# Local attention: the order of a head group's score matmuls on TensorE, and the place of its products with V

## The reference

```python
def local_attention(q, k, v):
    # 16 heads of 64; windows of 32 queries see the window before and their own
    bk2, bv2 = (look(bk), look(bv))
    mask = (it < jb) | (it > jb + w) | (jb == -1)
    sim = jnp.einsum('bhwie,bhwje->bhwij', bq, bk2) * QK_SCALE
    sim = jnp.where(mask, -jnp.finfo(sim.dtype).max, sim)
    attn = jax.nn.softmax(sim, -1)
    return jnp.einsum('bhwij,bhwje->bhwie', attn, bv2)

def attn_layer(x, Wqkv, qs, ksc, Wo):
    q, k, v = jnp.split(x @ Wqkv, 3, -1)
    # l2norm of q and k, scales, rotary tables, local_attention
    return out @ Wo

for i in range(DEPTH):
    x = attn_layer(shift_tokens(x), ...) + x
    x = ffn_layer(shift_tokens(x), ...) + x
```

## Time and profile before

| | us |
|---|---|
| median of 3 runs | 2675.11 (2673.16 to 2679.03) |
| the profiled execution | 2671.8 |
| its span | 2669.9 |
| TensorE busy | 2478.0 (93%) |
| VectorE busy | 1932.8 (72%) |
| ScalarE busy | 1742.4 (65%) |
| GpSimd busy | 1552.0 (58%) |
| granted clock of TensorE | 0.983 of full |

### The profile page before, as it was taken

How to read it: one execution, slowest core, us unless ns; L and a number is a source line. 1 busy time by engine, 2 the same in 40 slices (tenths; PEclk the granted TensorE clock), 3 DMA queues, 4 the chain that set the end, 5 groups by cost and what they waited for, 6 DMA issues and landing times.

```text
span 2669.9 us, 62150 instructions
## 1 busy us (share of the span) xinstructions
PE 2478.0 (93%) x22737; PEld 1645.5 (62%) x22737; DVE 1932.8 (72%) x2966; ACT 1742.4 (65%) x3296; POOL 1552.0 (58%) x1359
## 2 busy tenths in 40 slices
PE   6898699996999999999999999999999999999995
PEld 3555366663666666666666666666666666666664
DVE  4899777775777777777777777777777777777773
ACT  5888454443666766667667676676666766667663
POOL 4787523333666666566656666666656666666661
PEclk8999899998999999999999999999999999999997
DMA  2312200000221221222212212122122221222211
GB/s 73 107 63 65 73 6 1 1 1 22 53 60 48 64 65 47 60 56 61 59 48 59 66 51 59 48 61 68 47 59 53 64 59 47 60 63 54 59 48 45
DMA packets 102906, 140.33 MB, mean 53 GB/s; under 512 B 63040, under 2 KB 63936, under 8 KB 102336
## 3 DMA queue, kind: packets, MB, share of 16 engines
q1 hardware_dynamic: 102848, 139.57, 19.5%
HBM read 56.39 MB, written 1.31 MB: 22 GB/s over the span
## 4 chain that ended last, share of the span: by engine, by line
issue 31%; POOL 26%; PE 11%; DVE 5%; ACT 1%; POOLq 1%; DMA 0%; DVEq 0%; SPq 0%; ACTq 0%
POOL f_qkr L1358 8%; POOL f_qkr L1365 5%; POOL f_Pr L1340 5%; POOL f_qkr L1357 5%; DVE f_m L1554 4%; PE f_psA L1723 4%; PE f_psD L1817 3%; POOL f_tab L1348 2%; PE f_psO L1707 2%; PE f_psP L1686 2%; ACT f_sq L1432 1%; POOL xall L1379 1%; POOLq L1348 0%; POOLq L1379 0%; PE f_psD L1727 0%
## 5 line engine op out<-in xcount | busy, mean ns | idle before, releaser
L1340 POOL TENSOR_TENSOR f_Pr<-f_Pr,f_rden 128x384 f32<-128x384 f32 x384 | 310.6, 829 | 696.4 <-DVE f_rden L1533 696.4
L1554 DVE TENSOR_TENSOR f_m<-f_psA,f_tab 128x1024 f32<-128x1024 f32 x384 | 452.5, 1220 | 245.7 <-ACT f_sq L1432 245.7
L1723 PE MATMUL f_psA<-f_W,f_xT 128*128 (+1 forms) x1152 | 605.2, 618 | 17.2 <-issue 10.5
L1365 POOL TENSOR_TENSOR f_qkr<-f_qkr,f_rn 128x1024 f32<-128x1024 f32 x192 | 360.9, 1900 | 0.3 <-DVE f_rn L1583 0.3
L1432 ACT ACTIVATE f_sq<-f_psA 128x512 f32<-128x512 f32 x384 | 228.8, 596 | 145.5 <-PE f_psA L1723 139.7
L1686 PEld LDWEIGHTS f_psP<-ident,f_Pr 128*96 128x96 f32 x1536 | 165.3, 126 | 218.9 <-POOL f_Pr L1340 152.3
L1407 ACT ACTIVATE f_PT<-f_psP 96x512 f32<-96x512 f32 x384 | 226.7, 590 | 86.3 <-PE f_psP L1686 74.9
L1357 POOL TENSOR_TENSOR f_qkr<-f_m 128x512 f32<-128x512 f32 x192 | 244.3, 1272 | 57.2 <-DVE f_m L1554 57.1
L1723 PEld LDWEIGHTS f_psA<-f_W,f_xT 128*128 128x128 f32 x1152 | 183.5, 196 | 141.5 <-issue 64.0
L1707 PE MATMUL f_psO<-f_PT,f_V 96*64 96x64 f32 x6144 | 263.8, 228 | 3.3
L1522 DVE TENSOR_REDUCE f_mx<-f_psS 128x8 f32<-128x768 f32 x192 | 179.7, 936 | 118.1 <-PE f_psS L1670 118.1
(11 more groups left out here) (160 smaller groups left out, 4440.2 us busy)
## 6 DMA issues: line engine op xcount, KB each, us to landing
f_V<-f_Vt SPq DMA_DIRECT2D x96, 384.0 KB, 4.2
f_V<-f_Vt SPq DMA_DIRECT2D x96, 256.0 KB, 3.5
f_W<-in_f_W SPq DMA_DIRECT2D x48, 344.0 KB, 3.0
m_Cb<-m_BC_rows SPq DMA_DIRECT2D x64, 256.0 KB, 3.2
f_W<-in_f_W SPq DMA_DIRECT2D x48, 296.5 KB, 3.6
f_V<-f_Vt SPq DMA_DIRECT2D x48, 128.0 KB, 4.5
f_xsA<-xall SPq DMA_DIRECT2D x97, 32.0 KB
f_xsA<-xall SPq DMA_DIRECT2D x97, 31.8 KB
```

The costliest lines, as they stand in the source:

```text
L1340: pool.tensor_tensor(pv, pv, rv.unsqueeze(3).broadcast_to([P, 2, 2, KEYS]), ALU.mult).then_inc(Pr_ready[g][j], 1)
L1365: pool.tensor_tensor(qv, qv, rn[:, j * H:(j + 1) * H].unsqueeze(2).broadcast_to([P, H, DH]), ALU.mult).then_inc(qkr_ready[j], 1)
L1554: dve.tensor_tensor(m12[:, j, :, half].rearrange("p m (h d) -> p m h d", d=DH), psA[n % 2][:, :].rearrange("p (h d) -> p h d", d=DH).unsqu ...
L1723: pe.matmul(psA[n % 2][:, :], xT[:, t, :], weights(i, W_QKV + n * 512, 512), start=True, stop=True).then_inc(A_full[n_fill], 1)
```

## The change

In `scores`, the loop over the four columns of heads is now outside the loop over the row halves: after two matmuls (both halves of the queries) on the lower 64 rows come two on the upper 64, and so on, in place of eight on the lower rows and then eight on the upper. The matmuls are the same. In `slot`, `times_v(1, 0)` moves behind `transpose_qk(0)`, right ahead of `times_v(1, 1)`; and `times_v(0, 0)` moves behind the W2 products of the odd slots, right ahead of `times_v(0, 1)`. Each moved call takes its waits along.

```diff
@@ -1662,9 +1662,9 @@
                     for par in range(2):
                         pe.matmul(psS[:, par, 0:GH // 2 * KEYS], identb[:, :], maskb[:, q, :, :].rearrange("p c k -> p (c k)"), start=True, stop=False, skip_group_check=True)
-                    for par in range(2):
-                        r = slice(par * DH, par * DH + DH)
-                        for c in range(4):
+                    for c in range(4):
+                        for par in range(2):
+                            r = slice(par * DH, par * DH + DH)
                             for half in range(2):
                                 k0 = half * HQ
                                 ins = pe.matmul(S4[half * HQ:(half + 1) * HQ, par, c, :], qT[r, q, 4 * g + c, k0:k0 + HQ],
@@ -1760,11 +1760,11 @@
                 if "C" in stages:
                     transpose_probs(1, 1)
-                    times_v(1, 0)
                 if "B" in stages:
                     pe.wait_ge(qkr_ready[0], v + 1)
                     transpose_qk(0)
                 if "C" in stages:
+                    times_v(1, 0)
                     times_v(1, 1)
@@ -1804,7 +1804,6 @@
                 if "B" in stages:
                     transpose_probs(0, 1)
-                    times_v(0, 0)
                 if "E" in stages:
                     weights_here(pe, i - 2, share_of(W_COLS))
                     pe.wait_ge(h01_ready, (i - 1) * 2)
@@ -1818,6 +1817,7 @@
                     ins.then_inc(w2_full, 1)
                 if "B" in stages:
+                    times_v(0, 0)
                     times_v(0, 1)
```

## The result

The changed kernel takes 2705.2 us (median of 4 runs, 2704.11 to 2708.71) against 2674.1 us for the kernel before in the same runs: ratio 1.0118, 95% interval 1.0098 to 1.0137. It is 31 us slower. Its profiled execution has a span of 2702.3 us, 32.4 us more than that of before. The forecast was 26 us more, and a range from 2686 to 2728 us.

The account below looks back on a forecast made before the run. Two latency chains across engines, not TensorE, were taken to bound the kernel. Terms of 0.46 + 0.46 - 0.38 = 0.54 us per pair, over 48 pairs, add 25.9 us to 2675.1: 2701 us, range 2686 to 2728 us.

Parts of the forecast that it names:

- two chains of latencies: Odd slot after the first scores, even slot from the gate products: waits across engines set the time, TensorE's work lies inside.
- The first pass moved behind the transposes of q and k: Second head group's products, both slots: first transposes stay, joined pass takes 1.08 us, everything behind starts 0.46 us later.
- Even slot: the whole 0.46 us reaches the next slot: Late gate products delay ScalarE's GELU table load and all behind it, so the next slot starts 0.46 us later.
- Scores: 0.82 us in place of 1.20, and it counts once: Alternating row halves save 0.38 us per set; only the odd slot's first of four sets per pair shortens the time.
- The tie of ScalarE in the odd slot: Later evacuations of products and k on ScalarE may delay the odd slot's first scores by 0 to 0.1 us; taken as 0.
- The tail: End of odd slot, products with V exchanged with W2: bounds -0.05 and +0.23 us per pair, taken as 0.
- The likeliest case: The main forecast, 0.54 us more per pair, chance 0.64; spans 2693 to 2712 us with its near bounds.
- (b): Rival at the odd slot's end: the loop's branch is not hidden, 0.77 us per pair, 2712 us; chance 0.07.
- (a): Rival on the scores: they don't overlap more, 0.92 to 1.21 us per pair, 2719 to 2733 us; chance 0.12.
- (c): Rival in the even slot: its 0.46 us delay is absorbed in a wait, 0.08 us per pair, 2679 us; chance 0.08.
- (d): Rival: TensorE is the bound, all four score sets count, -0.60 us per pair, 2646 us; chance 0.09.

Follow-up runs that it names:

- one set against three: Kernel before, scores alternating only in the odd slot's first set: 2655.3 us; only in the other three sets of a pair: 2674.0 us.
- the undone tail: Changed kernel with the odd slot's first pass of first-group products ahead of W2 again, as before: 2693.9 us, ratio 1.0079.
- the products alone: Changed kernel with the score loops in their old order, so only the products with V move: 2723.8 us, ratio 1.0184.
- the one set alone: Kernel before, scores alternating only in the first head group's set of the odd slots: 2655.3 us, ratio 0.9936.
- W2 last: Kernel with only the scores alternating, plus both passes of first-group products ahead of W2 in the odd slot: 2748.3 us, ratio 1.0297.

## Why the prediction was right

**What bounds the kernel.** Held. The prediction put the times on two chains of latencies and not on TensorE, and the test of one set against three shows it: 0.38 us per pair, 18 us, against nothing, for a third of the work.

**The first pass moved behind the transposes of q and k: +0.46 us in each slot.** The transposes stayed, the gap is empty, the joined pass is 1.08 us to the hundredth. The second transposes are 0.44 to 0.46 us later. The rule that I took from the Trainium skill, TensorEngine Tiling (Array Packing) (Key Properties), that a change of the tiling mode drains the engine, agrees with it: 1.08 us, not 1.24. The rival is that each new group of matmuls pays for filling the pipeline. The trace of the kernel before speaks against it. First the last transpose of a group and the first gate product behind it, then the last transpose and the first product with V.

```profile
1518.68 0.27 PE L1717 MATMUL f_psA<-ident,f_qkr 128*128 128x128 f32 x1
1518.79 0.38 PE L1727 MATMUL f_psD<-f_xnT,f_W 128*85 128x256 f32 x1
...
1517.47 0.27 PE L1717 MATMUL f_psA<-ident,f_qkr 128*128 128x128 f32 x1
1517.68 0.27 PE L1707 MATMUL f_psO<-f_PT,f_V 96*64 96x64 f32 x1
```

A new group on 128 rows follows the transpose after 0.11 us, which is also the distance of two transposes in a group; the products of 96 rows and 64 columns follow after 0.20 us, in all 87 places between 800 and 2600 us. So a new group alone costs nothing here, and the entry into the other shape of matmul costs 0.09 us. What the engine does in it, the trace does not show.

**Even slot: the whole 0.46 us reaches the next slot.** Held: the table load is 0.46 us later, and the gate product moved into the gap takes 0.31 of it back, so this is shown and not only argued. With the gate product out of the way, ScalarE's evacuations of the late products and of the keys hold the load next; they too are 0.46 us late by the same move.

**Scores: 0.82 us in place of 1.20, and it counts once.** Held in both parts: 12 in flight, and 0.38 us of the first set in the odd slot back, 18 us of 48 pairs, with nothing that can be told for the other three.

**The tie of ScalarE in the odd slot (0 to 0.1 us, taken as 0).** The pair of the undone tail is 0.50 us over that of before, where 0.46 + 0.46 - 0.38 = 0.54 stood, so the tie adds nothing.

**The tail: taken as 0, bounds -0.05 to +0.23 us.** This term was mis-sized: it is 0.20 us per pair, 10 to 11 of the 31 us. The step that failed was "a longer queue of matmuls ahead of the branch should hide it": the joined pass starts 1.30 us ahead of the next slot (1584.40 to 1585.70, in the tail shown above), where 1.08 would do, so 0.22 us of the loop's end stay bare. W2 also starts 0.97 us behind the probabilities, not 0.93. With both, the sum of the tail is 0.97 + 1.53 + 1.08 + 0.22 = 3.80 us, as measured, against 3.60 before. Why a pass of 1.08 us hides only 0.07 us of the loop's end, while W2 of 1.5 us hides all of it, is not settled; how far TensorE's own sequencer gets ahead of the matmuls would tell, and no run here measures it by itself.

**The total.** With the tail put in, the sum is 0.54 + 0.20 = 0.74 us per pair (0.73 in the two timelines, 0.71 as a mean over the loop). Times 48 that is 34 to 36 us; the spans differ by 32.4 and the medians by 31. The traces show where the rest went: the 47 distances from pair to pair are 33.2 us longer together, the stretch ahead of them, whose work is the same, is 2.1 us shorter, and the one behind them 1.3 us longer. So it is in part luck that the time lies as near to the forecast of 26 us as it does: the pair is 0.71 us longer where 0.54 stood.

One figure of the forecast does not follow from its own terms. The likeliest case with its near bounds (the tie at 0 to 0.1, the tail at -0.05 to +0.23 us) is 0.49 to 0.87 us per pair, so 2699 to 2717 us and not 2693 to 2712. The range of 2686 to 2728 us holds either.

**The rivals.** (b), the branch not hidden, is what happened on top of the likeliest case, with 0.71 us per pair where (b) said 0.77; it had a chance of only 0.07, at 2712 us, so the likeliest case came true in all its terms but the tail. (a), (c) and (d) are refuted: by the 12 in flight, by the products alone (+51 us), and by the three sets (no gain).

No kernel of the study is clearly faster than the one with the scores alone changed, 0.64% under the kernel before; the one set alone gives the same.

## What to carry to other kernels

An engine that is busy 93% of the time need not be the limit: much of its work can be filler, done while another engine sets the time. Before moving its work, ask for each place what ends the wait that follows: here one set of scores in four was worth 18 us and the other three nothing. A piece of work that stands just ahead of a wait is free where it is. Moved behind the wait, it lengthens the path, however busy the engine was before: here by 0.46 us of the 0.62 that it took alone. And where a chain of small steps crosses engines, look at who else is at work at its new time, not only at what it waits for.

## What the runs showed of the hardware

Matmuls on 64 rows of the lower and of the upper partitions, in different banks of PSUM, stream side by side if they are written near each other: 0.65 us from the first start to the last, in place of 1.03, for 32 instructions when they alternate by one or two matmuls, 0.70 by four. With eight in a row, the starts in the trace keep the rhythm of one half until 0.40 us, when ten of its sixteen instructions have started, and only then come the second half's.

The loop's end costs TensorE 0.29 us or more behind a single pass of 16 instructions, 0.22 behind a joined pass of 32, and nothing behind W2's twelve of 1.44 us together.

VectorE's `f_hatC` (a TENSOR_SCALAR of 128x128), where GpSimd is at work as it starts, ends shortly after GpSimd's running instruction does. In the changed kernel, at the odd slot's end:

```profile
1584.34 1.61 POOL L1340 TENSOR_TENSOR f_Pr<-f_Pr,f_rden 128x384 f32<-128x384 f32 x2 [2.75 <-DVE f_rden L1533]
...
1584.88 0.42 DVE L1599 TENSOR_TENSOR xall<-f_psD,xall 128x256 f32 x1 [0.62 <-PE f_psD L1816]
...
1585.22 0.82 DVE L1604 TENSOR_SCALAR f_hatC<-f_xsC,f_momC,f_rstdC 128x128 f32<-128x128 f32 x1
...
1585.91 1.90 POOL L1365 TENSOR_TENSOR f_qkr<-f_qkr,f_rn 128x1024 f32<-128x1024 f32 x1
```

GpSimd's instructions end at 1585.95, `f_hatC` at 1586.04. In the run with W2 last GpSimd's first of two ends near 1515.9 and `f_hatC` at 1515.98, 1.74 us after its start. In each of the twelve traces here, `f_hatC` starts 46 or 47 times while a GpSimd instruction runs, and it ends 0.08 to 0.09 us behind that one, whether it then lasts 0.62, 0.82 or 1.74 us (three times GpSimd goes over to its next instruction just then, and `f_hatC` ends behind the next). The other 49 or 50 times no GpSimd instruction runs as it starts, and it lasts 0.30 to 0.35 us. No wait in the trace joins the two. The Trainium skill, SBUF — State Buffer (Who interferes with whom), says that VectorE and GpSimd share one pair of ports, which is locked for a whole instruction, and lists tensor_scalar among the operations that can need it; by that rule `f_hatC` waits until GpSimd's instruction is through, and these ends agree with it. The 0.08 us left behind GpSimd's end are less than the 0.30 us that it takes alone, so a part of its time must pass before or during the wait. The ports were not tested by themselves.
